# Four banks for the inner values, and the end of the routing written out by itself, in a fused attention and mixture-of-experts kernel

## The reference

```python
B, T, D, H = (8, 1024, 256, 64)                 # 16 blocks of 512 tokens
...
x = layernorm(x) modulated -> phi(q), phi(k), v -> causal linear attention -> x + gate * out
h = layernorm(x) * (1 + scale) + shift
logits = layernorm(h) @ router_w.T + router_b   # top 2 of E = 8, softmax over the two
y = gelu(layernorm_e(h) @ w1[e] + b1[e]) @ w2[e] + b2[e]
out = x + gate * sum of the two weighted y
```

## Time and profile before

| | us |
|---|---|
| median of three runs | 1141.53 (1140.14 to 1142.62) |
| the profiled execution | 1140.76 |
| its span | 1139.0 |
| PE busy | 991.4 (87%) |
| DVE busy | 874.9 (77%) |
| ACT busy | 629.8 (55%) |
| POOL busy | 575.4 (51%) |

### The profile page before, as it was taken

One profiled execution on the slowest core, in us unless ns is written; L12 is line 12 of the kernel. 1 busy time (PEld: TensorE's weight loads), 2 busy tenths in 40 slices (PEclk: granted clock), 3 DMA queues, 4 the chain that ended last, 5 costly groups with the idle time before them and its releaser, 6 DMA issues.

```text
span 1139.0 us, 32684 instructions
## 1 busy us (share of the span) xinstructions
PE 991.4 (87%) x8083; PEld 793.3 (70%) x8084; DVE 874.9 (77%) x2878; ACT 629.8 (55%) x1356; POOL 575.4 (51%) x479
## 2 busy tenths in 40 slices
PE   5878889887467788888999999999999999999986
PEld 2545565555456666666888888888888888888864
DVE  7779998887867677667877778787777878777875
ACT  3668877765656656664454454545445454544553
POOL 3125766676575355553545454454545445454442
PEclk8889988888569999999999999999999999999999
DMA  5333544333875675754444454544434444444442
GB/s 173 90 90 122 165 153 131 131 113 116 217 217 144 121 166 107 170 86 95 62 79 72 68 84 76 93 75 83 74 66 77 74 82 72 77 82 77 79 76 36
DMA packets 172037, 118.92 MB, mean 104 GB/s; under 512 B 111900, under 2 KB 158664, under 8 KB 171960
## 3 DMA queue, kind: packets, MB, share of 16 engines
q0 software_dynamic: 32832, 54.88, 24.2%
q1 hardware_dynamic: 139128, 63.13, 23.5%
HBM read 78.01 MB, written 45.98 MB: 109 GB/s over the span
## 4 chain that ended last, share of the span: by engine, by line
PE 52%; DVE 7%; issue 6%; ACT 5%; SPq 1%; ACTq 0%; POOLq 0%; DVEq 0%; DMA 0%
PE banks L1533 26%; PE banks L1545 25%; DVE store L1184 2%; ACT xT L694 2%; ACT store L731 1%; ACT gf L702 1%; DVE xT L1379 1%; DVE store L1440 1%; DVE store L1438 1%; DVE rowbuf L1416 1%; DVE rowbuf L1426 1%; DVE nhl L1386 1%; ACT store L709 1%; SPq L431 0%; SPq L437 0%
## 5 line engine op out<-in xcount | busy, mean ns | idle before, releaser
L1533 PE MATMUL banks<-nhl,store 128*128 128x256 bf16 (+1 forms) x3408 | 454.6, 269 | 48.6 <-ACT gf L702 26.0
L1545 PE MATMUL banks<-store 128*128 (+1 forms) x3240 | 450.4, 274 | 8.6 <-DVE store L1440 8.0
L702 ACT ACTIVATE gf<-banks,b1t 128x256 f32<-128x256 f32 (+1 forms) x568 | 255.4, 460 | 353.7 <-PE banks L1533 341.0
L641 POOL DMA_INDIRECT out<-rowbuf,ydst x135 | 226.4, 1677 | 362.0 <-DVE rowbuf L1426 324.0
L1533 PEld LDWEIGHTS banks<-nhl,store 128*128 (+1 forms) x3408 | 318.5, 98 | 113.8 <-issue 64.4
L1545 PEld LDWEIGHTS banks<-store 128*128 128x128 bf16 x3240 | 307.9, 98 | 60.6 <-issue 13.7
L1440 DVE TENSOR_TENSOR store<-gf,store 128x256 bf16<-128x256 f32 (+1 forms) x568 | 233.8, 412 | 69.7 <-ACT store L709 52.7
L1438 DVE CAST store<-gf 128x256 bf16<-128x256 f32 (+1 forms) x492 | 146.9, 299 | 118.8 <-ACT gf L702 98.2
L599 POOL DMA_INDIRECT lists<-store,slot x128 | 137.5, 1074 | 80.0 <-DVE store L1117 45.8
L607 POOL DMA_INDIRECT csB<-y_rows,ygb x135 | 138.9, 1029 | 41.9 <-issue 41.9
L694 ACT ACTIVATE xT<-xT,gb 128x256 f32<-128x256 f32 (+1 forms) x142 | 76.0, 582 | 31.6 <-DVE xT L1379 29.7
(11 more groups left out here) (247 smaller groups left out, 1041.7 us busy)
## 6 DMA issues: line engine op xcount, KB each, us to landing
vk<-lists SPq DMA_DIRECT2D x256, 64.0 KB
b2t<-in_L_ffn_b SPq DMA_DIRECT2D x71, 128.0 KB
store<-in_L_attn_x SPq DMA_DIRECT2D x16, 512.0 KB, 5.2
out<-store SPq DMA_DIRECT2D x16, 512.0 KB, 3.2
store<-in_L_ffn_w SPq DMA_DIRECT2D x28, 256.0 KB
store<-in_L_ffn_w SPq DMA_DIRECT2D x7, 1024.0 KB, 8.5
csB<-mod_rows SPq DMA_DIRECT2D x16, 256.0 KB, 4.3
csB<-y_rows,ygb POOLq DMA_INDIRECT x135, 3.7
```

The source lines that it names most:

```text
L641: g.indirect_dma_start(out_rows, bass.IndirectOffsetOnAxis(ap=ydst[:, r, h:h + 1], axis=0), yt[:, r, h, :], None, compute_op=ALU.add).then ...
L702: a.activation(gf[:, c % 4, 0:halves(j) * P], hidden(j)[c % 2][:, 0:halves(j) * P], ACT.Gelu, bias=b1t[:, r, c:c + 1]).then_inc(gf_s, 1)
L1533: last = t.matmul(hidden(j)[c % 2][:, 0:halves(j) * P], w, nhl[:, r, m, 0:halves(j) * P], start=n == 0, stop=n == 5)
L1545: last = t.matmul(ACC[r][h][:, 0:D], g[:, c, h * P:(h + 1) * P], w, start=c == 0 and n == 0, stop=c == NI - 1 and n == 2)
```

## The change

The pipeline now ends after step 15, and what steps 16 to 20 did is written out per engine. The inner values get four banks. ACT's work on the next rows is cut in three pieces, behind gelus 1, 2 and 3, and is done in tile 0 for tile 1 too. The parts of the second expert are split in tiles 0 and 1, and the splits of the others follow. SP's program is unchanged.

```diff
+        LOG_END = V[:, 0:NC * E]
-        MM = bank[6:8]
-        MM0 = bank[4:6]
+        MM = (bank[0], bank[1], bank[6], bank[7])
...
-            for i in range(NB + 5):
+            for i in range(NB):
...
-        SPLITS = (1, 1, 1, 1, 1, 2, 2, 2, 2, 2, 2, 2, 2, 1, 2)
+        SPLITS = (2, 2, 1, 1, 2, 2, 2, 2, 2, 2, 2, 2, 2, 2, 2)
...
-            return 2 + k // 4, k % 4 // 2, k % 2
+            return 1 + k // 4, k % 4 // 2, k % 2
```

POOL (`placed` waits for a block's slots and scatters the given chunks, two DMAs each):

```diff
+            placed(NB - 5, (0,))
+            inverse_root(NB + 1, 1)
+            placed(NB - 5, (1, 2, 3))
+            inverse_root(NB + 2, 0)
+            inverse_root(NB + 3, 1)
+            placed(NB - 4, range(NC))
+            placed(NB - 3, range(NC))
+            pool.wait_ge(gb_out, 16)
+            pool.wait_ge(h2_s, NB)
+            gb_rows(0, 0)
+            placed(NB - 2, range(NC))
+            gb_rows(1, 1)
+            placed(NB - 1, range(NC))
```

ACT (`head_rows` is cut in `scale_rows`, one k each, and `head_rows`; `normed`, `routed`, `turned` and `differences` hold the former stages' instructions for block b):

```diff
-                    if c == 1 and not (isinstance(j, int) and (j == 0 or j + 1 >= TILES)):
-                        head_rows(j + 1, half + r, 1 - r)
+                    if not (isinstance(j, int) and j + 1 >= TILES):
+                        if c in (1, 2):
+                            scale_rows(j + 1, 1 - r, c - 1)
+                        if c == 3:
+                            head_rows(j + 1, 1 - r)
...
+            normed(NB - 3)
+            differences(NB - 5)
...
+            routed(NB - 4)
...
+            turned(NB - 4)
+            normed(NB - 2)
+            routed(NB - 3)
+            turned(NB - 3)
+            normed(NB - 1)
+            differences(NB - 4)
+            routed(NB - 2)
+            for n in range(2):
+                head_of(0, 0, n)
+            turned(NB - 2)
+            head_of(0, 1, 0)
+            routed(NB - 1)
+            differences(NB - 3)
+            head_of(0, 1, 1)
+            turned(NB - 1)
+            differences(NB - 2)
+            for k in range(NK):
+                scale_rows(0, 0, k)
+            head_rows(0, 0)
+            differences(NB - 1)
```

DVE (`early_part(n)` is `early_tiles` cut in eight; `modulated` is L999, L1002 and their statistics; `logits` adds the router's bias):

```diff
+                    if c == 0 and first:
+                        placed(NB - 1)
...
-                    if c == 3 and not first and not last_tile:
+                    if c == 5 and not last_tile:
                         split_rows(j + 1, half + r, 1 - r)
...
+            placed(NB - 5)
...
+            modulated(NB - 3)
+            moments(NB + 2, stats_before(NB + 1))
...
+            neg_mean_rstd(NB + 1, 1)
...
+                early_part(c)
...
+                early_part(NC + c)
+            logits(NB - 4)
+            modulated(NB - 2)
+            moments(NB + 3, stats_before(NB + 2))
+            absent_ranks()
+            neg_mean_rstd(NB + 2, 0)
+            highest(NB - 4)
+            choose(NB - 4, 0)
+            logits(NB - 3)
+            dve.wait_ge(nm_s, NB + 4)
+            modulated(NB - 1)
+            moments(NB + 4, stats_before(NB + 3))
+            placed(NB - 4)
+            neg_mean_rstd(NB + 3, 1)
+            highest(NB - 3)
+            choose(NB - 3, 1)
+            logits(NB - 2)
+            highest(NB - 2)
+            placed(NB - 3)
+            choose(NB - 2, 0)
+            turn(0, 0, 0)
+            picked(NB - 2)
+            for n in range(2):
+                rest_of(0, 0, n)
+            split_rows(0, 0, 0)
+            logits(NB - 1)
+            highest(NB - 1)
+            choose(NB - 1, 1)
...
+            destinations(0, 0, 0)
+            for n in range(2):
+                rest_of(0, 1, n)
```

PE (`ranked` are the matmuls of L1613 to L1618; after block 15's scores and P.V):

```diff
-                wait_past(pe, gf_s, NI * j + c - 1)
+                wait_past(pe, gf_s, NI * j + c - 3)
...
+            ranked(NB - 5)
...
+            turned(NB - 4)
...
+            last.then_inc(owo_s, 1)
+            logits(NB - 4)
+            absent_ranks()
+            turned(NB - 3)
+            logits(NB - 3)
+            ranked(NB - 4)
+            turned(NB - 2)
+            logits(NB - 2)
+            ranked(NB - 3)
+            turned(NB - 1)
+            ranked(NB - 2)
+            logits(NB - 1)
             first_early_waits()
             for c in range(NI):
+                if c == 1:
+                    ranked(NB - 1)
+                if c == 3:
+                    pe.wait_ge(lg_s, NB)
+                    pe.wait_ge(rest_s, 4)
+                    pe.wait_ge(base_s, NB)
+                    hold(pe, "pe")
                 tile_chunk(0, 0, 0, True, own, own, c)
```

More of the change, by code:

```diff
@@ new lines, in _ @@
+            neg_mean_rstd(NB + 1, 1)
+            dve.wait_ge(rden_s, NB)
+            for c in range(NC):
+                last = v.scalar_tensor_tensor(rows(NB - 1)(c), SO[c][:, 0:D],
+                                              rden[:, c:c + 1], rows(NB - 1)(c), ALU.mult, ALU.add)
+                if c + 1 == NC:
+                    last.then_inc(x2_s, 1)
+                early_part(c)
+            dve.wait_ge(nm_s, NB + 3)
+            dve.wait_ge(x2_s, NB)
+            hold(dve, "dve")
@@ new lines, in _ @@
+            for c in range(NC):
+                last = v.bn_stats(st[:, 1, c, :], rows(NB - 1)(c))
+                if c + 1 == NC:
+                    last.then_inc(st_s, 1)
+                early_part(NC + c)
[8 more added lines that the diff above has]
+            dve.wait_ge(nm_s, NB + 4)
@@ new lines, in ranked @@
+            def ranked(b):
+                pe.wait_ge(ohs_s, b + 1)
+                pe.wait_ge(x2_s, min(b + 4, NB))
+                flat = ohs[:, :, :].rearrange("p c e -> p (c e)")
+                pe.wait_ge(base_s, b)
+                hold(pe, "pe")
+                t.matmul(RANK.rearrange("p (c e) -> p c e", c=NC), onesf[0:1, 0:P], base[0:1, :].unsqueeze(1).to_broadcast([1, NC, E]), start=True, stop=False)
+                t.matmul(RANK, before[:, :], flat, start=False, stop=False)
+                for back in range(1, NC):
+                    t.matmul(O[:, back * E:NC * E], allone[:, :], flat[:, 0:(NC - back) * E], start=False, stop=back == NC - 1)
+                for c in range(NC):
+                    last = t.matmul(TOT, allone[:, :], flat[:, c * E:(c + 1) * E], start=c == 0, stop=c == NC - 1)
+                last.then_inc(rank_s, 1)
@@ new lines, in _ @@
+            pe.wait_ge(phi_s, NB)
+            pe.wait_ge(vT_s, NB)
+            pe.wait_ge(x2_s, NB - 1)
+            pe.wait_ge(lg_s, NB - 4)
+            pe.wait_ge(q2_s, NB)
+            for s in range(NC):
+                at = slice(0, H) if s % 2 == 0 else slice(H, 2 * H)
+                q_of = qk if s % 2 == 0 else q2
+                last = t.matmul(SC[s], vT[at, 1, s // 2 * P:(s // 2 + 1) * P], q_of[at, 1, s * P:T], start=True, stop=True)
+            last.then_inc(score_s, 1)
+            ranked(NB - 5)
@@ new lines, in _ @@
+            last.then_inc(pv_s, 1)
+            turned(NB - 4)
+            pe.wait_ge(strip_s, NB)
+            pe.wait_ge(qz_s, NB)
+            pe.wait_ge(oT_s, NB)
+            pe.wait_ge(wog_s, NB)
+            for c in range(NC):
+                last = t.matmul(SO[c][:, 0:D + 1], oz[:, 1, c * P:(c + 1) * P], wog[:, 1, :], start=True, stop=True)
+            last.then_inc(owo_s, 1)
[3 more added lines that the diff above has]
+            logits(NB - 3)
```

232 lines of the change are left out of this document (156 added, 76 removed).

## The result

The changed kernel took 1101.03 us, median of 4 runs (1100.62 to 1105.90), beside 1141.84 for the kernel before in the same runs: ratio 0.9654, 95% interval 0.9625 to 0.9684, a gain of 39.5 us by the ratio (40.8 by the medians). I had forecast 1116 us, a gain of 25.1, with a range of 1099 to 1130. The profiled execution has a span of 1099.5 us.

What follows compares the result with a forecast made beforehand. It took a DVE-ACT-DVE circle to pace tiles 0 to 14; 11.0 us saved through tile 6, 8.0 in tiles 7 to 13, -0.8, loop 3.4, half tiles 3.5 make 25.1 off 1140.76, forecast 1116, range 1099 to 1130.

Steps and rivals of the forecast that it cites:

- The routing's end: Before the expert tiles: first matmul at about 315, 14.6 us earlier; 10.1 us left at tile 1's first difference on DVE.
- The scatters: POOL's scatters end as before, delaying SP's loads; tile 3's gelu starts at 361, 2.2 us lost to this wait.
- The wait at tile 7: SP's load of expert 5's second part delays tile 7's bias: tile 6 takes 18.2 us for 14.42, 3.8 lost.
- Heads in pieces on ACT: Written-out tiles: DVE's idle of 3.54 us becomes 2.39, a tile with two splits takes 12.04 us, 1.15 less.
- The 0.77 us 'issue' at each turn of the loop stays: PE's 24 gaps at the loop's turns remain, since they are there without a bank wait; no saving counted.
- Splitting the rows on DVE moves from chunk 3 to 5 ... so nothing: DVE's later row split gains nothing, since the next tile needs it only at its start.
- My own sign of being wrong: The forecast is wrong if, among other signs, the loop's span changes by more than 6 us.
- the issue gaps close: Rival, 7%: two chunks more of freedom let PE's queue pass the loop's register read; 14 us more, 1102 us.
- Banks: Four banks save 3.4 us in the loop and 3.5 in the half tiles, 6.9 in sum, bounds 0 and 20.
- The low clock: Rival, 4%: PE falls to 1.2 GHz in the tiles, 21 us a tile against 12; three undo the gain (1143).

Runs made afterwards that it cites:

- before_four_banks: The kernel before with only the four banks added, from tile 2 on (chunk c waits for gelu c-4): 1141.96 us, ratio 0.9992.
- after_two_deep: The changed kernel with TensorE's chunk c waiting for the gelu of chunk c-2 again, as with two banks: 1102.95 us, ratio 0.9644.
- after_again: The changed kernel unedited, run on another chip: 1140.07 us, ratio 0.9884 to the kernel before.
- after_bias_7_again: Repeat of the changed kernel with tile 7's loads ahead of expert 5's second part in SP's queue: 1134.04 us, ratio 0.9840.

## Why the prediction was right in sign and near in size

*The routing's end: right.* First matmul 315, measured 314.69; block 15's nm 305, measured 304.10 (L973); block 15's ranks to 317.5, measured from 317.08; chunk 3 at 321, measured 321.33:

```profile
314.69 1.46 PE L1697 MATMUL banks<-nhl,store 128*128 128x256 bf16 x6
317.08 0.60 PE L1876 MATMUL banks<-base,onesf 1*128 1x32 f32 x2 [0.92 <-DVE ohs L1148]
...
321.33 1.01 PE L1697 MATMUL banks<-nhl,store 128*128 128x256 bf16 x4 [0.76 <-DVE base L1183]
```

Tile 1's first difference came at 334.53 for 334.2 forecast; of the 10.1 us ahead 9.7 came. But on the other two chips nothing of it was left.

*The scatters: right in kind, too small.* I let the last of them start at 351 to 352; it started at 354.25, and SP, which waits for its landing, issued rows 4 only from 359.52 and the bias of tile 3 at 364.09. The gelu started at 365.34, not 361:

```profile
354.25 0.99 POOL L595 DMA_INDIRECT lists<-store,slot  x1 [0.30 <-issue]
...
364.09 0.09 SPq L453 DMA_DIRECT2D b1t<-b_folded  x1
...
365.34 0.47 ACT L720 ACTIVATE gf<-banks,b1t 128x256 f32<-128x256 f32 x1 [5.53 <-issue]
```

*The wait at tile 7: right in kind, too small.* ACT waits 7.21 us where I said near 5, and the turn another 2.06 for the gains: 5.3 us lost in this tile for 3.8. I had counted the load of expert 5 as the thing that delays, and not that the gains for the turn stand behind the rows too. Moving tile 7's loads ahead gave 6 us back on either of the other chips, which shows the queue's order as the cause.

*Heads in pieces on ACT: right in the tiles.* Tiles 8 to 12 at 12.04 us with 2.39 us of idle; measured 12.3 and 2.36, here at tile 6:

```profile
407.49 0.70 DVE L1445 STREAM_TRANSPOSE xT<-vk 128x512 f32<-128x512 f32 x1
410.56 0.43 DVE L1506 TENSOR_TENSOR store<-gf,store 128x256 bf16<-128x256 f32 x1 [2.36 <-ACT store L727]
```

*The step that failed: "The 0.77 us 'issue' at each turn of the loop stays", and with it "Splitting the rows on DVE moves from chunk 3 to 5 ... so nothing".* I argued that the gap is there without a bank wait, which is so, and stopped at the word "issue", as if it were a fixed cost of the loop. It is a wait with two parts: the sequencer's 2.07 us, and the moment from which they run, the difference of chunk 4. I had priced the split by who needs its output (the next tile), not by what stands behind it on DVE. My own sign of being wrong was met: the loop's span was not to change by more than 6 us, and it changed by 27.8. The rival "the issue gaps close" named the right effect, at 0.6 us a turn where the trace of before loses 0.94 (1.60 from group to group for 0.66), and the wrong cause: held to two chunks they stay closed, with four banks and the old order they stay open. That its 1102 us is nearly the 1101.03 measured is luck, since the written-out tiles gave 9.7 us less than either sum has and the loop some 10 more. So is, in part, that my range held: its core of 1110 to 1122 missed, and it reached down to 1099 only to take in the rivals beside it.

*Banks: 6.9 us were forecast, and the runs show about none* (0.9 ± 2.3 us from before_four_banks, and nothing clear of noise from after_two_deep). In the first the half tiles gain the 0.5 us each that I priced. The 0.07 us a tile that I priced in the loop do come, but not from the banks: a tile behind no gap takes 10.57 us before and in before_four_banks, 10.48 with ACT's work in pieces, also in after_two_deep. What I set against the banks held: the Trainium skill, "TensorE: Matmul & The Clock Gate", section "HAM oscillation — how this bites in real kernels", reports for another kernel no further gain from PSUM double-buffering. The runs agree here, with 0.9992.

*The low clock* cost little: 0.97 in the tiles for 0.98.

## What to carry to other kernels

A gap called "issue" at a loop's turn is a deadline: measure from the last wait that the engine's sequencer had to pass to the first instruction behind the turn. If that time is the same at every turn, the work that releases that wait is what to move earlier, on another engine if need be; here one digit on DVE was worth 17 us, where the new end of the routing with the old order was worth nothing. And where an instruction on a shared in-order engine is moved, price also what stands behind its old place. In a DMA queue written by hand, put the loads of the next tile ahead of one that waits for a later event.

## What the runs showed of the hardware

- TensorE's sequencer takes 2.05 to 2.12 us from the last wait of the loop's body to the first matmul of the next turn, with a branch (0.22 us) and one register read of three entries (0.77 us) in it. A read of one entry takes 0.30, and three of them are 0.37 us more than the one of three. It all hides if the wait is met early enough.
- The same program differs by chip: 1101 us and 1140 us (two chips), while the kernel before differs by 11 to 13. Most of the added time lies in written-out code, where semaphores that PE raises come up to 12 us after the modelled end of their matmuls; in the loop some are 1.0 to 1.2 us late, and it loses 0.1 us a tile. One can't say from one chip what a change is worth where it rearranges long written-out stretches.
- In a trace in which a third of the semaphore events is missing (14,850 for 21,650), "issue" may stand for a wait whose releaser was not recorded: one and the same wait of ACT reads 14.67 us "<-issue" in after_again and 14.06 "<-remote" in after_bias_7_again.
